# A state-space decoder kernel on one core: which state indices hand one of their four accumulations to ScalarE and GpSimd

## The reference, cut to what matters

```python
def step(state, inp):
    dt_t, B_t, C_t, u_t = inp
    dA = jnp.exp(dt_t[..., None] * A)
    state = state * dA + (dt_t * u_t)[..., None] * B_t[:, None, :]
    y = jnp.einsum('bdn,bn->bd', state, C_t)      # the sum over 16 states n
    return (state, y)
...
y = ys.transpose(1, 0, 2) + x * D
y = y * jax.nn.silu(gate)
return y @ W_out.T
```

## Time and profile before

| what | value |
|---|---|
| median of 3 runs | 3014.36 us (3012.97 to 3014.8) |
| the profiled execution | 3013.76 us |
| its span, first to last instruction | 3011.6 us |
| PE busy | 2738.4 us, 91% |
| DVE busy | 2549.7 us, 85% |
| POOL busy | 1925.6 us, 64% |
| ACT busy | 1693.9 us, 56% |
| mean granted TensorE clock | 0.963 |

### The profile page before, as it was taken

One profiled execution on the slowest core, in us unless ns is written; L12 is line 12 of the kernel. 1 busy time (PEld: TensorE's weight loads), 2 busy tenths in 40 slices (PEclk: granted clock), 3 DMA queues, 4 the chain that ended last, 5 costly groups with the idle time before them and its releaser, 6 DMA issues.

```text
span 3011.6 us, 35283 instructions
## 1 busy us (share of the span) xinstructions
PE 2738.4 (91%) x11120; PEld 1565.7 (52%) x11120; DVE 2549.7 (85%) x3521; ACT 1693.9 (56%) x2848; POOL 1925.6 (64%) x884
## 2 busy tenths in 40 slices
PE   8968899999989999998999887888889999999996
PEld 4535555555555555555555454455544555555553
DVE  2359899999999999999999999999957777777775
ACT  2347566565655657566565654655625555555553
POOL 1159897888969888896988987989822122122121
PEclk9989899999999999999999998999899999999998
DMA  5432323534242343424333332322311121121110
GB/s 175 133 100 81 100 90 102 144 89 135 84 157 91 109 135 100 123 88 152 111 92 92 99 91 89 126 83 74 98 42 64 56 70 49 56 70 49 56 63 21
DMA packets 132876, 281.32 MB, mean 93 GB/s; under 512 B 12528, under 2 KB 12656, under 8 KB 132224
## 3 DMA queue, kind: packets, MB, share of 16 engines
q1 hardware_dynamic: 132736, 279.59, 30.2%
HBM read 245.86 MB, written 33.69 MB: 93 GB/s over the span
## 4 chain that ended last, share of the span: by engine, by line
PE 54%; DVE 31%; issue 9%; ACT 5%; POOL 1%; DMA 0%; DVEq 0%; POOLq 0%; ACTq 0%; SPq 0%
DVE arena L1259 17%; PE banks L473 15%; PE banks L497 9%; DVE arena L1275 7%; PE banks L567 7%; PE banks L703 4%; PE banks L660 4%; PE banks L616 3%; PE banks L641 3%; PE banks L510 2%; PE banks L671 2%; ACT banks L1020 2%; PE banks L631 2%; DVE arena L1215 1%; PE banks L710 1%
## 5 line engine op out<-in xcount | busy, mean ns | idle before, releaser
L1183 POOL TENSOR_TENSOR arena<-arena 128x2048 f32<-128x2048 f32 x256 | 1163.0, 4543 | 81.4 <-PE banks L567 81.4
L1259 DVE TENSOR_TENSOR_SCAN arena<-banks,arena 128x512 f32<-128x512 f32 x1024 | 1184.2, 1202 | 20.9 <-POOL arena L1183 17.9
L1020 ACT ACTIVATE banks<-arena,a_sb 128x508 f32<-128x508 f32 x1024 | 696.9, 684 | 734.5 <-DVE arena L1259 734.1
L473 PE MATMUL banks<-arena 128*128 128x512 f32 x2048 | 951.1, 602 | 11.3 <-DMA arena<-in_xT 8.4
L567 PEld LDWEIGHTS banks<-ident,arena 128*128 128x128 f32 x4096 | 493.5, 146 | 416.3 <-issue 194.7
L567 PE MATMUL banks<-ident,arena 128*128 128x128 f32 x4096 | 576.2, 284 | 136.7 <-DVE arena L1275 69.9
L473 PEld LDWEIGHTS banks<-arena 128*128 128x128 f32 x2048 | 372.4, 194 | 363.3 <-issue 360.2
L1275 DVE SCALAR_TENSOR_TENSOR arena<-banks,cg,arena 128x512 f32<-128x512 f32 x640 | 452.0, 736 | 70.7 <-PE banks L567 70.1
L497 PE MATMUL banks<-arena 128*128 128x512 f32 x1024 | 473.1, 601 | 5.6 <-DMA arena<-in_WoutT 4.3
L1129 POOL TENSOR_TENSOR arena<-arena 128x512 f32<-128x512 f32 x240 | 306.9, 1279 | 203.3 <-ACT arena L848 201.9
L1196 POOL TENSOR_TENSOR arena<-arena 128x512 f32<-128x512 f32 x128 | 141.3, 1104 | 453.1 <-DVE arena L1431 453.0
(11 more groups left out here) (137 smaller groups left out, 2980.2 us busy)
## 6 DMA issues: line engine op xcount, KB each, us to landing
arena<-b_scratch SPq DMA_DIRECT2D x128, 512.0 KB, 5.1
arena<-in_WinX SPq DMA_DIRECT2D x128, 256.0 KB, 2.9
arena<-in_WinZ SPq DMA_DIRECT2D x128, 256.0 KB, 2.7
arena<-in_WoutT SPq DMA_DIRECT2D x32, 1024.0 KB, 5.6
u_scratch<-arena SPq DMA_DIRECT2D x64, 256.0 KB, 5.1
arena<-u_scratch SPq DMA_DIRECT2D x16, 1024.0 KB, 9.4
arena<-x_scratch SPq DMA_DIRECT2D x32, 512.0 KB, 3.5
arena<-in_xT SPq DMA_DIRECT2D x14, 1024.0 KB, 7.7
```

Of the source, the lines that this page charges most:

```text
L473: last = nc.tensor.matmul(home(kind, i), wr[w % 2][:, k, :], x[:, k, :], start=(k == 0), stop=(k == KC - 1))
L1020: nc.scalar.activation(by_seq(bank(i % 2))[:, :, 1:SEQ], by_seq(dt[s % 2][:, i, :])[:, :, 1:SEQ], ACT.Exp, scale=a_sb[:, QD * q + i, n:n + ...
L1183: nc.gpsimd.tensor_tensor(hb[n % 4].rearrange("p (i t) -> p i t", i=QD), dtu, brep[pair % 3][:, n % 2:n % 2 + 1, :].broadcast_to([P, QD, G ...
L1259: nc.vector.tensor_tensor_scan(h, bank(i % 2), h, 0.0, ALU.mult, ALU.add)\
```

## The change

The set of shared indices becomes a list by step. Steps 11 to 15 keep the five indices 0, 3, 6, 9, 12. Steps 0 to 10, those with X tiles, get the seven indices 0, 2, 6, 8, 10, 12, 14. So in each of the eleven steps turn 2 of indices 2, 8, 10 and 14 moves from VectorE to ScalarE and GpSimd, and turn 2 of indices 3 and 9 moves back to VectorE. The counts that waits compare with become running sums over the steps. (The short description of the change speaks of the third sequence: that is turn b = 2.)

```diff
--- before.py
+++ after.py
@@ -51,8 +51,9 @@
 OWN = GB - 1
 ONE = 1
 SPLIT = OWN - 1
-SHARED = (0, 3, 6, 9, 12)
-KEPT = OWN * N - len(SHARED)
+SHARED = [(0, 3, 6, 9, 12) if s >= NS - 5 else (0, 2, 6, 8, 10, 12, 14) for s in range(NS)]
+KEPT = [OWN * N * s - sum(map(len, SHARED[:s])) for s in range(NS + 1)]
+LENT = [sum(map(len, SHARED[:s])) for s in range(NS + 1)]
 
 
 LEAD = 5 * QD
@@ -88,12 +89,12 @@
 
 def kept(s, n, b):
 
-    return KEPT * s + OWN * n - sum(v < n for v in SHARED) + b + 1 - (b == SPLIT and n in SHARED)
+    return KEPT[s] + OWN * n - sum(v < n for v in SHARED[s]) + b + 1 - (b == SPLIT and n in SHARED[s])
 
 
 def shared(s, n):
 
-    return len(SHARED) * s + sum(v <= n for v in SHARED)
+    return LENT[s] + sum(v <= n for v in SHARED[s])
 
 
 def jobs():
@@ -559,7 +560,7 @@
                         after(pe, "part_ok", U)
                     elif b > 1:
                         pe.wait_ge(S["acc_ok"], kept(s, n, b - 2))
-                    elif U and (n - 1) % N in SHARED:
+                    elif U and (n - 1) % N in SHARED[(U - 1) // N]:
                         pe.wait_ge(S["part2_ok"], shared((U - 1) // N, (U - 1) % N))
                     elif U:
                         pe.wait_ge(S["acc_ok"], kept((U - 1) // N, (U - 1) % N, SPLIT))
@@ -592,9 +593,9 @@
                     pe_ssm(pe, (LEAD + QD * s) // 2)
                 pe_filler(pe, s, 2 * n + 1)
 
-            pe.wait_ge(S["acc_ok"], KEPT * (s + 1))
+            pe.wait_ge(S["acc_ok"], KEPT[s + 1])
             pe.wait_ge(S["sum_ok"], (N - 1) * (s + 1))
-            pe.wait_ge(S["sum2_ok"], (len(SHARED) - 1) * (s + 1))
+            pe.wait_ge(S["sum2_ok"], LENT[s + 1] - s - 1)
             for i in range(QD):
                 pe_room(pe, "Y", QD * s + i)
                 y = home("Y", QD * s + i)
@@ -850,14 +851,14 @@
 
         def act_part2(act, s, n):
 
-            k = SHARED.index(n)
+            k = SHARED[s].index(n)
             act.wait_ge(S["t_done"], QD * (N * s + n) + SPLIT + 1)
             if k == 0:
                 after(act, "yt_mm", QD * s)
                 act.wait_ge(S["cg_ok"], s // NQ + 1)
                 dst = acc2
             else:
-                after(act, "sum2_ok", (len(SHARED) - 1) * s + k - 2)
+                after(act, "sum2_ok", LENT[s] - s + k - 2)
                 dst = part2[:, k % 2, :]
             nc.scalar.activation(dst, bank(2), ACT.Identity, scale=cg[:, SPLIT, n:n + 1])\
                 .then_inc(S["part2_ok"], 1)
@@ -1022,7 +1023,7 @@
                                          scale=a_sb[:, QD * q + i, n:n + 1]).then_inc(S["exp_ok"], 1)
                     act_between(act, s, n, i)
                 if U >= 2:
-                    if (U - 2) % N in SHARED:
+                    if (U - 2) % N in SHARED[(U - 2) // N]:
                         act_part2(act, (U - 2) // N, (U - 2) % N)
                     act_part(act, (U - 2) // N, (U - 2) % N)
 
@@ -1129,11 +1130,11 @@
             nc.gpsimd.tensor_tensor(v, v, part[:, n % 2, :], ALU.add).then_inc(S["sum_ok"], 1)
 
         def pool_sums2(pool, s, n):
-            k = SHARED.index(n)
+            k = SHARED[s].index(n)
             if k == 0:
                 return
             pool.wait_ge(S["part2_ok"], shared(s, n))
-            after(pool, "sum2_ok", (len(SHARED) - 1) * s + k - 1)
+            after(pool, "sum2_ok", LENT[s] - s + k - 1)
             nc.gpsimd.tensor_tensor(acc2, acc2, part2[:, k % 2, :], ALU.add).then_inc(S["sum2_ok"], 1)
 
         def pool_u(pool, m):
@@ -1158,7 +1159,7 @@
                 U = N * s + n
                 if U >= 4:
                     pool_sums(pool, (U - 4) // N, (U - 4) % N)
-                    if (U - 4) % N in SHARED:
+                    if (U - 4) % N in SHARED[(U - 4) // N]:
                         pool_sums2(pool, (U - 4) // N, (U - 4) % N)
                 if n == 1 and s > 0:
                     pool_z(pool, Z - 1)
@@ -1270,7 +1271,7 @@
             if fresh:
                 last = nc.vector.tensor_scalar(acc[:, b, :], bank(2 + b % 2), c, None, ALU.mult)
             else:
-                before = n - 2 if b == SPLIT and n - 1 in SHARED else n - 1
+                before = n - 2 if b == SPLIT and n - 1 in SHARED[s] else n - 1
                 dve.wait_ge(S["acc_ok"], kept(s, before, b))
                 last = nc.vector.scalar_tensor_tensor(acc[:, b, :], bank(2 + b % 2), c, acc[:, b, :],
                                                       ALU.mult, ALU.add)
@@ -1350,16 +1351,16 @@
 
         def dve_step(dve, s):
             if s % NQ == 0:
-                after(dve, "acc_ok", KEPT * s)
+                after(dve, "acc_ok", KEPT[s])
                 after(dve, "part_ok", N * s)
-                after(dve, "part2_ok", len(SHARED) * s)
+                after(dve, "part2_ok", LENT[s])
                 nc.vector.tensor_copy(cg[:, :, :], ssn[:, :, R + N:SS]).then_inc(S["cg_ok"], 1)
             for n in range(N):
                 U = N * s + n
 
                 for part in range(2):
                     for b in range(2 * part, min(2 * part + 2, OWN)):
-                        if b != SPLIT or n not in SHARED:
+                        if b != SPLIT or n not in SHARED[s]:
                             dve_acc(dve, s, n, b)
                     if U + 2 < N * NS:
                         for i in (2 * part, 2 * part + 1):
@@ -1688,7 +1689,7 @@
             pool_z(pool, QD * NS - 1)
             for n in range(N - 4, N):
                 pool_sums(pool, NS - 1, n)
-                if n in SHARED:
+                if n in SHARED[NS - 1]:
                     pool_sums2(pool, NS - 1, n)
             pool.wait_ge(S["fin"], QD * NS)
             nc.gpsimd.memset(ones, 1.0).then_inc(S["ones_set"], 1)
```

## The result

The changed kernel takes 3047.1 us in the median of 4 runs (3040.82 to 3048.28), against 3014.27 before; the ratio is 1.011, with a 95% interval of 1.0096 to 1.0124. Forecast were 3044 us and a range of 3027 to 3053. The profiled execution took 3046.03 us, its span is 3043.9: 32.3 more than before.

A forecast was written before the change was run, and what follows sets the result against it. The prediction took POOL's queue ahead of the sum of index 15 to set each step's end. POOL's tail and smaller terms, 19.2 us, plus 11 for the clock made 30 on 3013.76: 3044 us, range 3027 to 3053.

The forecast's parts named there:

- POOL's queue in front of the last sum: End of each step: Y tiles start 1.36 to 1.38 us after POOL's sum of index 15 starts, so POOL's queue releases them.
- The tail's size: Steps 1, 2, 4, 6, 8, 10: 2.46 us of POOL additions less 0.58 waits plus 0.24, so 2.12 each, 12.7 together.
- the 0.24 through VectorE: Up to index 6, DVE is 0.24 us later because index 3 returns; PE and POOL's sum of index 6 follow.
- Steps 3 and 7: POOL's 1.64 us wait for the sum of index 9 swallows the sum for 8: 0.82 us slower each, 1.6 together.
- Step 0: End of step 0: no POOL waits to absorb the added sums, so 2.46 + 0.24 = 2.70 us slower.
- The layer-norm steps: Steps 5 and 9: PE's 3.46 us wait for DVE after the statistics shrinks by 0.75, leaving 1.37 slower each, 2.7 together.
- The clock: Y tiles at ten ends, steps 1 to 10: longer PE waits halve the pace, up to 1.64 us each; 11, bounds 0 to 13.9.
- VectorE's relief: 22 fewer accumulations, 14.1 us at most: 0.5 off PE's wait at index 11, 0.75 in steps 5 and 9, 0.5 in step 11.
- ScalarE at nothing: ScalarE's 22 added parts, 14.7 us, fit its gaps behind DVE's scans: no cost, unless gaps close, then up to 0.67 a place.
- rival 1: VectorE bounds the kernel, PE and POOL following it: the change gives back 14.1 us, 3000 us; chance 0.06.
- rival 2: Step ends grow by POOL's tail, 19.2 us, but PE's longer waits leave its pace alone: 3033 us; chance 0.20.
- Rivals 3 and 4: 3: added POOL work hidden, 3014 us, chance 0.05. 4: late bm starves scans or ACT's gaps close, 3060 us, 0.09.

The follow-up runs named there:

- the two pairs: Seven against five indices, sum of index 15 ahead of the third bm: 3002.38 and 3010.24 us; with the cg copy on ScalarE too: 2997.9 and 3004.96.
- the set with 7: The kernel before with shared indices 0, 2, 7, 9, 12 in steps 0 to 10, only the set changed: 3029.7 us, ratio 1.0057.

## Why the prediction was right

**The bound was POOL's queue in front of the last sum: right for the changed kernel, shown.** The distance from that sum to the Y tiles is 1.35 to 1.40 at the ends of steps 0 to 14 after the change, under waits from 0.75 to 6.92. Two additions late in the queue cost 34 us, two early ones nothing. For the kernel before I said too much. In its even steps the last sum waited 0.41 for ScalarE's part, and taking the product in front of it away left them at 126.35 to 126.37. My sum is not touched by that, since it took this wait off as slack.

**The tail's size, 2.12 a step in six steps: right.** It was 2.16 to 2.21. Both parts can be read off: 68.80 instead of 66.91 from the sum of index 6 on (1.89 for 1.88), and that sum, less the slower Y tiles, came 0.28 later in step 8, for the 0.24 through VectorE. Steps 3 and 7 gave 0.74 and 0.75 for 0.82. Step 0 was under-sized, 3.9 for 2.70. Some 50 us into it POOL was already 1.4 behind, where I had 0.24 at most; what caused that no run separates.

**The layer-norm steps: mechanism right.** In step 9 PE's wait there fell by 0.66 (3.45 to 2.79) where I had 0.75. In step 5 it fell from 3.46 to 1.83, since its Y tiles had taken 2.9 longer and part of that came out of the wait:

```profile
867.55 1.31 PE L568 MATMUL banks<-ident,arena 128*128 128x128 f32 x8 [1.83 <-DVE arena L1276]
```

Steps 5 and 9 together lost 1.8 where I had 2.7.

**The clock: mechanism right, the term too small.** I took 80% of ten falls, 11 us, with 13.9 as the bound. All ten came, behind waits of 2.96 to 3.34 (forecast 2.9 and 3.4), and the Y tiles took 4.4 to 6.0 instead of 3.13: 16.1 us, or 15.3 with the end of step 0, whose Y tiles took 0.8 less. My bound was wrong as a bound: 1.64 came from one row, and behind the end of step 4 the loss was 2.9. The onset between 1.89 and 2.63 was wrong too, for pace fell behind waits of 1.72 and 2.00 elsewhere. That the median came out 3 us above the forecast is this term, less what steps 12 and 13 gained: the fall at the end of step 11 did not come this time, behind the same wait of 2.63, and the wait at the end of step 12 was then 0.75 instead of 2.40. That part was luck.

**VectorE's relief: under-sized, without effect on the sum.** I gave it the wait before the projection and the starts of steps 5, 9 and 11. The first was right: that wait shrank from 1.24 to 0.70. I gave nothing for the end of a step. With the tail out of the way ScalarE's last part, and with it the end, comes 0.6 sooner in even steps, and in all the relief is 7 to 8 us (7.9 and 7.1 in the two pairs). In the change as made it could not show there, since POOL set the ends.

**ScalarE at nothing: right for this set, not in general.** The even steps came out within 0.1 us of the sum without it. Index 7 showed what it costs when the cover is gone: about 0.9 us a step.

The rivals: VectorE as the bound (rival 1) was false for the change; its 14 us are about twice what the relief is worth with the tail gone. The tail without the clock (rival 2) is the run with TensorE kept busy: 3027 where I had 3033, since the falls in steps 3 and 7 were missing from it and the kernel before, measured beside it, was 3 us lower. Rivals 3 and 4 are not borne out: the tail was not hidden, and of a late bm VectorE's wait in step 8 shows 0.7, ahead of an end that POOL set.

## What to carry to other kernels

Before moving work to a less busy engine, find what its queue releases last in each period and count what stands ahead of that, from its last idle moment on: an engine at 64% (87% in the loop) was the bound, and two 1.2 us additions a step cost 34 us or nothing by place. When a wait has "issue" as its name, look for an event at a constant distance ahead of it in several periods under different waits. Once such a tail is known, reordering is cheaper than unloading: one sum put ahead of one product, and a copy moved off its way, turned 1.1% slower into 0.5% faster.

## What the runs showed of the hardware

**A small copy on VectorE held up by GpSimd.** The 128x64 copy from SBUF to SBUF takes 0.18 us where POOL idles (27 times in nine kernels) and 3.33 when it starts 1.23 behind the start of POOL's 128x2048 product. All 21 copies that began while POOL was in an instruction (0.81 to 3.35 us long) ended 0.04 to 0.06 behind the end of that instruction. ScalarE did the same copy in 0.24 to 0.26 beside such instructions. The Trainium skill, page "SBUF — State Buffer", section "Who interferes with whom", says that a copy on DVE in a two-port mode and a GpSimd instruction exclude each other for the whole instruction, whichever starts first; these traces agree where POOL started first, and none has the other order or shows the copy's mode. VectorE's scans and accumulations, with one input in PSUM, kept their lengths beside the same products: in the kernel before the accumulations took 735 ns inside a product and 734 with POOL idle, the scans 1201 and 1205. That copy was no part of my working at all.

**The clock does not follow the length of a wait alone.** TensorE's pace fell behind all ten waits of 2.96 to 3.34 before the Y tiles (granted clock 0.69 over those at the end of step 8, 1.00 before the change; over the 6.0 us at the end of step 4 it is 0.50, which is 1.2 instead of 2.4 GHz all through), and behind all four of 2.34 to 2.40. Otherwise the same wait in the same place, behind the same work, did both:

- At the end of step 11 a wait of 2.61 to 2.63 occurs in nine of these kernels. The Y tiles took 4.6 to 4.8 in two of them (the kernel before and the set with 7) and 3.12 in seven.
- Some 44 us into steps 3 and 7 all fourteen kernels have a wait of 1.97 to 2.03, and the pace fell behind 19 of these 28.
- Before the projection at index 11 four kernels have a wait of 1.71 to 1.72 in eight steps each, and it fell behind 15 of the 32, though never in steps 2, 6 and 10. It did not fall behind the eight waits of 1.60 to 1.62 before Y tiles.

Such a fall costs about 1.3 to 1.7 us (the Y tiles above, 1.5 in steps 3 and 7). What decides it these runs do not show. A few falls more or less are of the size by which runs of one kernel differ, 7.5 us over four runs after the change and 6.0 over sixteen of the kernel before. With one trace of each kernel it is not shown that they are the reason.
